# First layer norm in groups of four tiles, turned into the scores' banks behind the first keys, with loads reordered

## The reference

```
x = x + cross_attention(layernorm(x), ctx)    # 16 heads, 256 keys per sequence, mask, times fside
x = x + self_attention(layernorm(x))          # 16 heads, 64 keys
x = x + expert_mean(layernorm(x))
x = x + cross_attention(layernorm(x), ctx)    # other weights, no mask
x = x + state_space(layernorm(x))
x = x + rms_norm_attention_and_moe(layernorm(x))
layernorm(x) = (x - mean(x)) / sqrt(var(x) + 1e-5)
```

## Time and profile before

| | us |
|---|---|
| median of 3 runs | 1098.29 |
| lowest and highest run | 1097.12, 1099.25 |
| profiled execution | 1096.61 |
| its span, from the first to the last instruction | 1094.7 |
| PE busy | 839.2 (77%) |
| DVE busy | 548.9 (50%) |
| ACT busy | 446.4 (41%) |
| POOL busy | 397.8 (36%) |
| mean granted clock of PE | 0.879 |

### The profile page before, as it was taken

One profiled execution on the slowest core, in us unless ns is written; L12 is line 12 of the kernel. 1 busy time (PEld: TensorE's weight loads), 2 busy tenths in 40 slices (PEclk: granted clock), 3 DMA queues, 4 the chain that ended last, 5 costly groups with the idle time before them and its releaser, 6 DMA issues.

```text
span 1094.7 us, 21754 instructions
## 1 busy us (share of the span) xinstructions
PE 839.2 (77%) x6944; PEld 590.6 (54%) x6944; DVE 548.9 (50%) x1397; ACT 446.4 (41%) x1527; POOL 397.8 (36%) x577
## 2 busy tenths in 40 slices
PE   1899989689879658888987462677453999999990
PEld 0666666478754226666665341566341466666660
DVE  2477777568744343655655577576432222222222
ACT  1566666346614224656564102466400233333320
POOL 3356465535458754243344534222425000000005
PEclk9999999899969888999998765777655999999995
DMA  8121112633241634343233200211167034443004
GB/s 320 42 56 46 49 48 65 237 104 109 88 154 46 196 105 136 104 137 106 96 106 123 97 0 12 86 40 40 49 229 279 16 132 153 145 140 131 16 21 120
DMA packets 63723, 114.37 MB, mean 104 GB/s; under 512 B 6304, under 2 KB 20384, under 8 KB 62880
## 3 DMA queue, kind: packets, MB, share of 16 engines
q1 hardware_dynamic: 55488, 103.15, 28.0%
q10 hardware_dynamic: 6624, 6.03, 1.7%
q0 software_dynamic: 1536, 4.20, 1.3%
HBM read 79.02 MB, written 34.34 MB: 104 GB/s over the span
## 4 chain that ended last, share of the span: by engine, by line
PE 45%; ACT 15%; DVE 15%; POOL 10%; issue 9%; DMA 4%; SPq 1%; DVEq 0%; ACTq 0%; POOLq 0%
ACT probs L1116 6%; PE ps L967 4%; PE ps L969 4%; PE ps L968 4%; PE ps L524 3%; ACT probs L1075 3%; PE ps L567 3%; PE ps L583 2%; DMA ctx_t<-in_ctx 2%; DVE stat L1478 2%; PE ps L990 2%; PE ps L992 2%; PE ps L991 2%; ACT probs L1066 2%; PE ps L979 2%
## 5 line engine op out<-in xcount | busy, mean ns | idle before, releaser
L1266 POOL TENSOR_TENSOR var<-mv,half 128x1 f32<-128x1 f32 x56 | 11.0, 196 | 288.5 <-DVE mv L1479 201.2
L1298 POOL TENSOR_TENSOR piece_out<-piece_in,piece_out 128x512 f16<-128x512 f32 x96 | 112.7, 1173 | 7.7
L1966 DVE TENSOR_TENSOR probs<-ps,ctx_t 128x512 f32<-128x512 f32 x46 | 29.6, 686 | 155.0 <-PE ps L969 155.0
L567 PE MATMUL ps<-pack_const,probs 128*128 128x128 f32 x512 | 78.7, 291 | 28.8 <-DVE vbuf L1520 11.3
L1461 POOL DMA_INDIRECT pt<-y_rows,neg x16 | 15.4, 962 | 234.2 <-DMA y_rows<-vbuf 229.7
L1323 POOL TENSOR_TENSOR probs<-probs,gp 128x512 f32<-128x512 f32 x64 | 81.3, 1303 | 51.1 <-ACT probs L1066 51.1
L567 PEld LDWEIGHTS ps<-pack_const,probs 128*128 128x128 f32 x512 | 58.7, 146 | 53.2 <-DVE vbuf L1520 13.1
L1297 POOL CAST piece_out<-piece_in 128x512 f16<-128x512 f32 x96 | 62.2, 648 | 41.9 <-DMA piece_in<-in_w 40.7
L967 PE MATMUL ps<-arena,qbuf 128*128 x184 | 71.0, 386 | 0.0
L968 PE MATMUL ps<-arena,qbuf 128*128 x184 | 70.8, 385 | 0.0
L969 PE MATMUL ps<-arena,qbuf 128*128 x184 | 70.8, 385 | 0.0
(11 more groups left out here) (246 smaller groups left out, 2000.3 us busy)
## 6 DMA issues: line engine op xcount, KB each, us to landing
piece_in<-in_w SPq DMA_DIRECT2D x96, 256.0 KB, 2.8
w_parts<-piece_out SPq DMA_DIRECT2D x96, 256.0 KB, 2.0
arena<-w_parts SPq DMA_DIRECT2D x8, 3072.0 KB, 12.6
ctx_t<-in_ctx SPq DMA_DIRECT2D x32, 256.0 KB, 2.7
x_rows<-piece_out SPq DMA_DIRECT2D x1, 2944.0 KB, 16.7
qbuf<-x_rows ACTq DMA_DIRECT2D x23, 128.0 KB, 2.5
y_rows<-vbuf ACTq DMA_DIRECT2D x23, 128.0 KB, 1.7
arena<-in_xa SPq DMA_DIRECT2D x2, 1282.0 KB, 7.1
```

What stands on the lines that cost most here:

```text
L567: last = pe.transpose(AB[:, o:o + P], pr[:, 2 * c + n, kt * P:(kt + 1) * P], ident)
L1298: pool.tensor_tensor(both[:, PIECE:], src, both[:, 0:PIECE], ALU.subtract).then_inc(piece_split, 1)
```

## The change

- SP loads x in two halves of four tiles, each with its own semaphore, then const and xa0, then the contexts of sequences 0 and 1 and the masks of 0; sa, ffn, four and ssm follow at step 1, behind these and ahead of the third context.
- DVE waits for the first half of x alone, takes the stats of four tiles one behind another and then their aggregates, the same for the second half, and then normalises all eight tiles into `xn_all`, each with a signal of its own. It waits for const only behind this.
- POOL takes epsilon and the power for four tiles in one instruction each.
- PE projects the keys of sequence 0 first, then turns all eight tiles into the four banks of S without waiting for ACT, then projects the first queries. In xa1 too the first keys come ahead of the first queries, with the wait for `xt_all` moved in front of both.
- ACT copies two turned tiles (128x512) at a time, four copies. They stand ahead of its copy of the first keys.

```diff
+        first_stats, first_mv = top[:, 0:48], logit[:, 0:16].rearrange("p (t n) -> p t n", n=2)
+        first_var, first_rstd = logit[:, 16:24], logit[:, 24:32]
...
-            sp.dma_start(x[:, :], t["x"]).then_inc(loaded["x"][0], 16)
-            for name in ("const", "xa0", "sa", "ffn", "four", "ssm"):
+            first = TILES * D // 2
+            sp.dma_start(x[:, 0:first], t["x"][:, 0:first]).then_inc(loaded["x"][0], 16)
+            sp.dma_start(x[:, first:], t["x"][:, first:]).then_inc(loaded["x_rest"][0], 16)
+            for name in ("const", "xa0"):
...
+                    if isinstance(k, int) and k == 1:
+                        for name in ("sa", "ffn", "four", "ssm"):
+                            sp.dma_start(W[name]["whole"], t[name]).then_inc(loaded[name][0], 16)
...
-            def ln_step(k, s, h):
-                hold(pe, G["ln"]["xt"], k)
-                turn_rows(G["ln"], k)
-            skewed(pe, TILES, 0, ln_step)
+            def turn_first_rows():
+                for i in range(TILES):
+                    hold(pe, G["ln"]["normed"], i + 1)
+                    for c in range(DC):
+                        last = pe.transpose(S[:, i * D + c * P:i * D + (c + 1) * P],
+                                            xn_all[:, i * D + c * P:i * D + (c + 1) * P], ident)
+                    last.then_inc(G["ln"]["turned"].sem, 1)
...
+                if st == "xa1":
+                    hold(pe, prev["xt"], TILES)
...
-                    if live(k, 0, SEQS):
+                    if isinstance(k, int) and k == 0:
+                        project_keys(k, s, h)
+                        if st == "xa0":
+                            turn_first_rows()
+                        project_queries(h)
+                    elif live(k, 0, SEQS):
...
-            skewed(act, TILES, 0, lambda k, s, h: copy_turned(G["ln"], k))
+            for i in range(0, TILES, 2):
+                hold(act, G["ln"]["turned"], i + 2)
+                act.activation(XT[:, :, i * P:(i + 2) * P].rearrange("p c (t n) -> p c t n", t=2),
+                               S[:, i * D:(i + 2) * D].rearrange("p (t c n) -> p c t n", t=2, c=DC), ACT.Copy)\
+                   .then_inc(G["ln"]["xt"].sem, 2)
...
-            def ln_step(k, s, h):
-                root_of_variance(G["ln"], k)
-                chain.restart()
-            skewed(pool, TILES, 0, ln_step)
+            for half_of in range(2):
+                r = slice(4 * half_of, 4 * half_of + 4)
+                hold(pool, G["ln"]["stats"], 4 * half_of + 4)
+                chain.link(pool.tensor_tensor(first_var[:, r], first_mv[:, r, 1], half[:, 1:2].broadcast_to([P, 4]), ALU.add))
+                pool.tensor_tensor(first_rstd[:, r], first_var[:, r], half[:, 0:1].broadcast_to([P, 4]), ALU.pow)\
+                    .then_inc(G["ln"]["rstd"].sem, 4)
+            chain.restart()
...
-            def ln_step(k, s, h):
-                tile_stats(G["ln"], k)
-                hold(dve, G["ln"]["turned"], k)
-                normalise(G["ln"], k, xn[:, :])
-                chain.restart()
-            skewed(dve, TILES, 0, ln_step)
+            for half_of in range(2):
+                dve.wait_ge(*loaded["x_rest" if half_of else "x"])
+                tiles = range(4 * half_of, 4 * half_of + 4)
+                for i in tiles:
+                    chain.mark(dve.bn_stats(first_stats[:, 6 * i:6 * i + 6], tile(x, i)))
+                for i in tiles:
+                    chain.join()
+                    dve.bn_aggr(first_mv[:, i, :], first_stats[:, 6 * i:6 * i + 6]).then_inc(G["ln"]["stats"].sem, 1)
+            for i in range(TILES):
+                hold(dve, G["ln"]["rstd"], 4 * (i // 4) + 4)
+                dve.tensor_scalar(tile(xn_all, i), tile(x, i), first_mv[:, i, 0:1], first_rstd[:, i:i + 1],
+                                  ALU.subtract, ALU.mult).then_inc(G["ln"]["normed"].sem, 1)
+            chain.restart()
+            dve.wait_ge(*loaded["const"])
```

More of the change, by code:

```diff
@@ L317, in build @@
         }
-        loads = {"first": ["x", "const"], "xa0": ["xa0"], "sa": ["sa"], "ffn": ["ffn"], "ssm": ["four", "ssm"],
+        loads = {"x": ["x"], "x_rest": ["x_rest"], "const": ["const"], "xa0": ["xa0"], "sa": ["sa"], "ffn": ["ffn"], "ssm": ["four", "ssm"],
                  "late": ["xa1", "la", "moe"]}
@@ L1468, in _ @@
             chain = Chain(dve, dve_chain)
-            dve.wait_ge(*loaded["x"])
-            dve.wait_ge(*loaded["const"])
             K = W["const"]
```

## The result

| | before | changed |
|---|---|---|
| median of 6 runs, us | 1098.22 | 1090.11 |
| lowest, highest | 1094.52, 1101.22 | 1087.79, 1091.67 |
| profiled execution, its span | 1096.61, 1094.7 | 1089.91, 1088.1 |

The ratio is 0.9925, with a 95% interval of 0.9902 to 0.9948: 8.1 us faster. The sign and the place of the gain are the forecast's; the size isn't: 12.4 us were predicted, and 1090.11 lies 0.7 above the range. Two more comparisons of the same pair gave 0.9906 (0.9878 to 0.9934) and 0.9914 (0.9886 to 0.9943). All 14 runs of the changed kernel have a median of 1089.1 and 46 of the one before 1098.2, so 9.1 is the better figure of the gain, and 3.3 us of the forecast are missing. (By this figure the time, 1089.1, would lie 0.3 inside the range.)

The account below looks back on a forecast made before the run. The start was taken as bound by waits: const, the norm's chain, then the third context. 11.5 us there plus 0.9 in xa1 make 12.4, from 1096.61 to 1084.2, with 1.7 for the runs' median 1085.9 us; range 1083.9 to 1089.4.

Parts of the forecast that it names:

- this mark: Start of the third keys in xa0: predicted at 28.4 instead of 39.89, 11.5 us sooner, all behind it following unchanged.
- Rival C: xa0's loop from the third keys on runs at a lower clock because PE waits: slower, 1114.7 us; chance 0.03.
- D: Whole kernel: a later wait, such as late weights of sa, hides the start; no change, 1098 us; chance 0.03.
- B: xa1: the keys-first order gains nothing there, leaving 11.5 us of gain, 1086.8 us; chance 0.07.
- rival A: Start: smaller gain, PE staying at 1.2 GHz (1088.7 us) or an instruction fetch in full queues (1088.2); chance 0.17.
- So keys(1) starts at 21.2: Start of xa0: second keys begin at 21.2 instead of 33.09, 11.9 us earlier.
- ACT copies four pairs at 0.61 and begins 0.6 after the first turns: Start: ACT's copies of the turned tiles take 2.4 us from 17.4, ending at 19.9 with steps between.
- One issue more costs SP about 0.45 us, hidden by the backlog: Start, SP's queue: loading x in two costs no time; the first context lands at 13.3, first keys start at 13.4.
- the clock: Start, PE: first keys take 3.4 us, part of it at the 1.2 GHz level; sixteen turns take 2.2.
- the third context takes some back: xa0: issued at 25.1 behind the weights, the third context lands at 28.3, so the gain is 11.5 us, not 12.0.
- the 0.5 of slack: xa0: second keys may start 0.5 us later at no cost, since the third context waits behind the weights.
- the swap in xa1: xa1: keys ahead of queries, ACT's copy running beside the queries, saves 0.9 us up to the third context's issue.

Follow-up runs that it names:

- table_early: Changed kernel, with ACT first copying one column of ones so that its table loads at the very start: 1085.16 us, ratio 0.9874 to the kernel before.
- whole_table: Changed kernel with x in one load again and ACT's table loaded early, both together: 1083.56 us, ratio 0.9859 to the kernel before.
- x_whole: Changed kernel with x in one load again and one wait for it: 1090.08 us, ratio 0.9913 to the kernel before.
- spaced: whole_table with four and ssm loaded behind the second context, sa behind the third, ffn behind the fourth: 1085.09 us, ratio 0.9868 to the kernel before.
- warm_whole: whole_table plus 34 unused matmuls of ones on PE before the first keys: 1087.9 us, ratio 0.9914 to the kernel before.
- warm_late_weights: warm_whole with sa, ffn, four and ssm issued behind the third context and second masks: 1094.72 us, ratio 0.9964 to the kernel before.
- spaced_const: spaced with const issued behind the first context and POOL's wait for it, cast and memset behind the powers: 1083.18 us, ratio 0.9866 to the kernel before.
- xa1_old: Changed kernel with queries ahead of the keys again in xa1 alone: 1087.8 us, ratio 0.9903 to the kernel before.
- again_after: Changed kernel run again unchanged, its second profile: span 1084.9 us, third keys at 29.32.
- again_after2: Changed kernel run a third time unchanged, its third profile: span 1087.4 us, third keys at 30.03.

## Why the prediction was right or wrong

**Right: where the gain comes from.** The start ended with the norm's chain, and taking keys and contexts in front of it moved the third keys by 10.6 us. Behind this mark xa0's loop is as long as before (137.9 to 138.2 us to its last keys in all six executions), and up to xa1 it is 372.7 us against 372.2 in the mean of three each. Rival C (slower by the loop's clock) is excluded by this, D (no change) by the ratio, and B (nothing from xa1) by the 9.84 against 8.74 us there. The measured 1089.1 lies nearest to rival A's 1088.7, but not by A's mechanism: the queries ran at full speed in all three executions, and most of the delay isn't the clock, as follows.

**The step that failed: "So keys(1) starts at 21.2".** It started at 23.4, 22.7 and 23.4. In the profiled execution the 2.2 us are 0.9 of landing, 1.3 of table load and 0.7 of clock, less 0.7, since the four copies took 2.06 us and not 2.5, and the second keys followed the queries after 0.99 and not 1.2. Three terms were thus wrong:

**Wrong, first: "ACT copies four pairs at 0.61 and begins 0.6 after the first turns".** It began 2.4 us after them. ACT's table load, 1.28 us, stood in the first trace at 0.74, where nobody waited, and the sum has no term for it. In the changed kernel it stands in front of ACT's first ACTIVATE and behind its wait. That this comes of ACT's first instruction being straight code now and not in the loop of before is the likely reason, but no run shows it; table_early shows that the load was on the path, and whole_table that without it the forecast's start comes.

**Wrong, second: "One issue more costs SP about 0.45 us, hidden by the backlog".** It isn't hidden, since const, xa0 and the first context all stand behind it: first keys at 14.3 and not 13.4, as x_whole shows (13.36). The later issue is about 0.47 of this (xa0 at 5.05 and not 4.58); what makes up the rest no run shows.

**Wrong, third: the clock.** I took 3.4 for the first keys; they took 3.75, 3.53 and 3.75 in three executions of the changed kernel, and the turns 3.18, 1.91 and 2.31 instead of 2.2. What counts of the turns is the first pair, after which ACT may begin: 1.15, 0.69 and 1.08 us instead of 0.6. This is part of rival A, which I gave 0.17.

**Right: "the third context takes some back".** By whole_table it lands at 28.6 although issued at 24.7, and spaced removes this. In table_early, whole_table and warm_whole it came 0.6 to 0.7 us behind the last weights, as the sum had it (0.6). In the changed kernel itself the term was masked: with second keys 2.2 late, the context was issued at 27.3 and landed in 2.9 us, near the bare 2.8, though the last weights came only at 28.5. The queue held up nothing there, and the 0.5 of slack that I counted on couldn't take up a delay of 2.2. warm_late_weights has 13.8 us for a context behind 5 MB. The rule that the Trainium skill, DMA: Bandwidth & Descriptors, section Queues, rings and completion order, gives, that each DMA engine takes a ring's descriptors in order, agrees with these landings.

**Wrong, fourth: the range, and what stays open.** Its edges came from one profiled execution of each kind of stretch. By the three profiles of each kernel 3.6 us of the forecast are missing (spans 1095.6 and 1086.8 in the mean). 0.9 are the mark: it came 1.4 later than forecast, by the step above, and the kernel before reached it 0.5 later than in the first trace. 0.4 are the swap in xa1 (9.67 to 9.16 in these six, where I had 0.9), and this is scatter, since all fourteen executions give 1.1. The other 2.3 lie in stretches that the change didn't edit: 0.5 between third keys and xa1, 1.8 behind xa1's third context (675.1 against 673.3, single values from 671.7 to 676.3). Of these 1.8, 1.6 come behind xa1's last keys (527.6 against 526.0). The eight other kernels with the new start differ there by as much, 525.5 to 528.4, with a mean of 527.1 over all eleven, so about 1 us may be the change's and no run settles it. The times agree with the marks no better: x_whole gained 9.2 us with a mark 9.7 sooner than the kernel before, whole_table 14.6 with 11.8, table_early 14.1 with 10.8. So of the 3.3 us by which the time misses the forecast the step above explains 0.9, and the cause of the rest is open. A range that took in the 3.5 us by which the stretch to xa1 differs between two executions of one kernel would have held the result.

## What to carry to other kernels

Where ACT's first instruction stands behind a wait, look whether its table load does too, as here at 19.00; a copy of one column at the very start took it to 0.74. Loads in the order of their use served here, but space them: a small load came 0.6 us behind the last bytes ahead of it, and 13.8 us behind its issue with 5 MB ahead, so large loads belong singly behind the small ones that a loop asks for. Both moved the third keys; their worth in the time of the whole kernel is not clear of the scatter. And before an effect of some us is summed up, take the same stretches from two or three executions of the unchanged kernel.

## What the runs showed of the hardware

The granted clock over the 67.9 us behind xa0's loop, code that no run edited, was 0.92 in three of the fourteen executions (before, warm_whole, spaced_const), 0.85 in one (xa1_old) and 0.80 to 0.82 in ten. With 0.92 the way from third keys to xa1 took 368.8 to 370.2 us, in the others 370.9 to 375.5 (385.8 with the late fourth context). PE, after 2.1 us without a matmul, ran eight matmuls in 2.08 us instead of 1.16 in one execution (x_whole), and after 2.2 us at full speed in three others (again_after, again_after2 and xa1_old, queries in 1.16). A power on four columns took POOL 1.05 to 1.14 us against 0.57 for one column. With a load of 1 MB split in two, what was queued behind it was first used 0.8 us later (14.5 against 13.7 in the means of five).
